# Edge-attribute loads of a graph layer: one group ahead in one burst, gated on the first scatter pair

## The reference, cut to what matters

```
row, col = edge_index                       # src, dst
tp  = fctp_messages(x[col], edge_attr, W1, W2, W3, W4)   # per edge: 160 features from x[col] and 32 attributes
messages = tp @ Wm + bm
agg = segment_sum(messages, row, num_segments=N_NODES)   # scatter-add over random src
upd = concatenate([x, agg], -1) @ Wu + bu
out = layernorm(x + x + upd)
```

## Time and profile before

| | |
|---|---|
| median of 3 runs | 1928.71 us (1927.19 to 1929.68) |
| the profiled execution | 1923.78 us, its span 1922.0 us |
| first scatter, last scatter, issued at | 139.77 us, 1679.95 us |
| DVE's first product (L493) of two groups 88 apart | 198.8 us, 1592.4 us |
| busy share of the span: PE, DVE, POOL, ACT | 86%, 81%, 56%, 47% |
| mean share of the DMA engines in use, loop | 0.76 to 0.79 |

### The profile page before, as it was taken

How to read it: one execution, slowest core, us unless ns; L and a number is a source line. 1 busy time by engine, 2 the same in 40 slices (tenths; PEclk the granted TensorE clock), 3 DMA queues, 4 the chain that set the end, 5 groups by cost and what they waited for, 6 DMA issues and landing times.

```text
span 1922.0 us, 35044 instructions
## 1 busy us (share of the span) xinstructions
PE 1660.2 (86%) x11964; PEld 894.9 (47%) x11964; DVE 1549.8 (81%) x1727; ACT 894.5 (47%) x1721; POOL 1079.2 (56%) x837
## 2 busy tenths in 40 slices
PE   5439999999999999999999999999999999378883
PEld 2214444444444444444444444444444444266662
DVE  6347888888888888888888888888888886089994
ACT  1204444444444444444444444444444444168885
POOL 3106666766666666666666666666666665301110
PEclk9779999999999999999999999999999999789997
DMA  9996777777777777777777777777777774799994
GB/s 378 405 377 181 232 232 226 231 230 230 230 228 231 231 230 231 229 230 231 235 234 236 235 237 234 237 225 239 239 234 235 231 230 99 237 361 420 418 412 178
DMA packets 174616, 490.06 MB, mean 255 GB/s; under 512 B 48664, under 2 KB 99096, under 8 KB 149484
## 3 DMA queue, kind: packets, MB, share of 16 engines
q1 hardware_dynamic: 91980, 379.42, 51.6%
q0 software_dynamic: 82304, 109.12, 27.3%
q10 hardware_dynamic: 288, 0.95, 0.2%
HBM read 393.10 MB, written 96.31 MB: 255 GB/s over the span
## 4 chain that ended last, share of the span: by engine, by line
DMA 39%; issue 20%; POOL 20%; PE 11%; DVE 5%; ACT 2%; SPq 1%; POOLq 1%; ACTq 0%; DVEq 0%
DMA agg<-summed,row_idx 25%; POOL agg L324 14%; POOL xg L307 6%; DMA prod<-agg 5%; DMA xg<-in_x_rows,dst_sb 4%; DMA agg<-start_rows 4%; PE ps L648 3%; PE ps L641 2%; DVE stats L585 2%; DVE prod L566 2%; DMA e_sb<-in_e_rep 1%; ACT spread L365 1%; PE ps L694 1%; PE ps L629 1%; PE ps L695 1%
## 5 line engine op out<-in xcount | busy, mean ns | idle before, releaser
L324 POOL DMA_INDIRECT agg<-summed,row_idx x392 | 642.2, 1638 | 448.9 <-DMA agg<-summed,row_idx 294.0
L505 DVE TENSOR_TENSOR prod<-ps,e_sb 128x2048 f32<-128x2048 f32 x294 | 663.7, 2285 | 136.8 <-PE ps L648 132.2
L648 PE MATMUL ps<-prod,packed_sb 128*32 128x512 f32 x3136 | 752.7, 603 | 0.8 <-ACT S_sb L377 0.8
L307 POOL DMA_INDIRECT xg<-in_x_rows,dst_sb x392 | 410.5, 1047 | 179.4 <-issue 117.8
L641 PE MATMUL ps<-prod,packed_sb 128*32 128x512 f32 x2352 | 394.3, 600 | 0.0
L365 ACT ACTIVATE spread<-xg 128x1536 f32<-128x1536 f32 x98 | 145.5, 1485 | 424.1 <-DMA xg<-in_x_rows,dst_sb 413.5
L513 DVE TENSOR_TENSOR prod<-ps,e_sb 128x3072 f32<-128x3072 f32 x98 | 328.1, 3348 | 0.0
L493 DVE TENSOR_TENSOR prod<-ps,e_sb 128x2048 f32<-128x2048 f32 x98 | 223.9, 2285 | 108.6 <-ACT A_sb L371 69.4
L648 PEld LDWEIGHTS ps<-prod,packed_sb 128*32 128x32 f32 x3136 | 148.6, 109 | 156.7 <-issue 156.7
L629 PEld LDWEIGHTS ps<-packed_sb,spread 128*128 128x128 f32 x1176 | 127.3, 143 | 172.2 <-issue 123.6
L377 ACT ACTIVATE S_sb<-ps 128x512 f32<-128x512 f32 x98 | 58.7, 599 | 277.8 <-PE ps L648 277.8
(11 more groups left out here) (62 smaller groups left out, 1748.6 us busy)
## 6 DMA issues: line engine op xcount, KB each, us to landing
e_sb<-in_e_rep SPq DMA_DIRECT2D x98, 1536.0 KB, 7.2
e_sb<-in_e_rep SPq DMA_DIRECT2D x98, 1024.0 KB, 5.6
agg<-start_rows SPq DMA_DIRECT2D x49, 640.0 KB, 17.1
prod<-agg SPq DMA_DIRECT2D x48, 640.0 KB, 10.7
out<-prod POOLq DMA_DIRECT2D x48, 640.0 KB, 7.7
row_sb<-in_src_row SPq DMA_DIRECT2D x98, 256.0 KB
prod<-in_x_t SPq DMA_DIRECT2D x25, 640.0 KB, 11.8
e_sb<-in_x_t SPq DMA_DIRECT2D x24, 640.0 KB, 12.9
```

The source lines that it names most:

```text
L307: nc.gpsimd.indirect_dma_start(xg[g[1] % 2][:, q, :], None, x_rows, bass.IndirectOffsetOnAxis(dst_sb[g[1]][:, q:q + 1].bitcast(U32), 0)).t ...
L324: nc.gpsimd.indirect_dma_start(agg, bass.IndirectOffsetOnAxis(row_idx[g[1]][:, q:q + 1].bitcast(U32), 0), summed[g[1]][:, q // 2, q % 2 * ...
L505: nc.vector.tensor_tensor(prod[g[1] % 2][:, 4 + 4 * i:8 + 4 * i, :].rearrange("p (a b) e -> p a b e", b=2), ps[:, t_bank(g, 1 + i), :].uns ...
L648: return nc.tensor.matmul(ps[32 * quarter:32 * quarter + 32, S_BANK, :], w[:, 32 * half:32 * half + 32], prod[g[1] % 2][:, tile, :], start ...
```

## The change

`load_e(g)` now is called for group s+1 in slot s, not for s+2, and only from slot 1 on (groups 0 and 1 are loaded ahead of the slots, as before). Its two transfers are issued one after the other with no wait between them. Ahead of the first stand a wait until DVE is through with group g-2, and from group 8 on a wait until the first pair of scatters of group g-4 has landed. For g = s+1 that is group s-3, the one whose scatters POOL issues in its slot s and whose `rows` DVE does in its slot s. Nothing else changes: the same transfers, the same sizes and buffers.

```
             def load_e(g):
                 if at_least(g, 2):
-                    sp.wait_ge(multiplied, number(g) * USES - 2 * USES + 4)
+                    sp.wait_ge(multiplied, (number(g) - 1) * USES)
+                    hold(sp, sp_passed)
+                if at_least(g, 8):
+                    sp.wait_ge(scattered, (number(g) - 4) * 64 + 32)
+                    hold(sp, sp_passed)
                 sp.dma_start(e_sb[g[1] % 2][:, 0:4, :], ...).then_inc(es_in[g[1]], 16)
-                if at_least(g, 2):
-                    sp.wait_ge(multiplied, number(g) * USES - 2 * USES + 6)
                 sp.dma_start(e_sb[g[1] % 2][:, 4:ET, :], ...).then_inc(ev_in[g[1]], 16)
...
-                if live(2):
-                    load_e(shift(s, 2))
+                if live(1) and at_least(s, 1):
+                    load_e(shift(s, 1))
```

## The result

| | before | after |
|---|---|---|
| median (lowest to highest), 4 runs each | 1927.95 us (1925.67 to 1929.68) | 2035.91 us (2032.3 to 2042.88) |
| ratio, 95% interval | | 1.0567 (1.0531 to 1.0604) |
| the profiled execution, its span | 1923.78, 1922.0 us | 2034.27, 2032.5 us |
| mean time of a group, from group 4 to group 94 | 15.79 us | 17.01 us |

What follows compares the result with a forecast made beforehand. POOL's scatter pairs, made long by attribute loads in flight, were taken to set the rate. The profiled execution summed to 1923.8 - 6 + 86 + 0 = 2004 us; the median, 4.9 us above, to 2010, range 1920 to 2055.

Steps and rivals of the forecast that it cites:

- steady term: Loop, 90 intervals of gated groups: a group takes 16.8 us instead of 15.84, +86 us (-31 to +140).
- the start: Before the loop: less load ahead of the last seven table pieces, so the first scatter goes earlier; -6 us (-12 to +10).
- The gate is what SP waits for last: SP's queue: the first pair of group s-3 always lands after `rows(s-3)`, for which `load_src` waits; the pair lands 5.3 us later.
- The loop through the gate costs nothing: Pair landed, load, `times_xs`, `rows`, POOL's restart, pair landed: 14.4 to 15.0 us, about the floor of 14.9.
- The burst is 0.8 us ahead of every second pair: SP issues both transfers 0.3 us after the first pair's landing, POOL the second pair at 1.1 us after it.
- Clear interval 6.42, hit interval 10.4: POOL's time from pair to pair: 6.42 us without a load, 10.4 (9.1 to 11.0) with both transfers on it.
- End, 0: Last scatter pairs: 16 `x_t` loads still fall on three of the last four pairs; 0 us (0 to +10).
- `times_xv` hides its load: DVE: the second transfer is through at 9.5 us after the landing, while PE holds DVE to 9 anyway; 1.9 us to spare.
- ACT's waits for gathers vanish: ACT: its waits for gathers go, since POOL must now be ahead; nobody gains, as PE then waits for DVE.
- No pair got in between the two transfers: Rival, second pair: scatters served between the burst's two transfers, interval 6.4 to 8, 1860 us; milder form 1885 to 1920; chance 0.18.
- The loop didn't bind: Rival: the gate's loop is longer than summed, PE's clock fall included; 17.5 us or more a group, 2070 and up; chance 0.07.
- The change moves nothing: Rival: gate long met when SP comes, or two pairs hit cost the same as one hit harder; 15.8 us, 1925; chance 0.05.

Runs made afterwards that it cites:

- e3: The changed kernel, but from group 8 on each transfer carries one attribute tile instead of four and six; 1832.87 us, ratio 0.9516.
- e10: The changed kernel with its gate on the landing of group g-4's second scatter pair instead of the first; 2518.56 us, one execution.
- e6: The changed kernel with DVE's `add_parts` cut to 8 of 512 columns, its sums left incomplete; 2039.67 us, ratio 1.0569 to the kernel before.
- e2: The changed kernel without the wait for the first scatter pair, `load_src` still ahead of the burst; 2073.36 us, ratio 1.0794.
- e5: The changed kernel without the wait for the first scatter pair, and with `load_src` called after `load_e`; 1972.59 us, ratio 1.0237.
- e1: The kernel before, two groups ahead and ungated, with both transfers waiting for the end of `times_y` and issued back to back; 1973.24 us, ratio 1.0246.
- e7: The kernel before, two groups ahead, with each transfer gated on a different scatter pair's landing and `load_src` between the two transfers; 1875.97 us, ratio 0.9733.
- e8: The changed kernel, its gate waiting for POOL's count placed behind a pair's second scatter instead of for a landing; 2131.14 us, ratio 1.1038.
- e11: The changed kernel, its gate waiting for POOL's count placed behind a pair of gathers instead of for a landing; 2193.22 us, ratio 1.1383.

## Why the prediction held, step by step

The sign and the place were right: 2036 us against 2010 in a range to 2055. Of the profiled execution it missed 30 us (2034.27 for 2004), 23 of them in the steady term and 6 at the start. The upper end of the range was drawn tighter than its own terms: with an interval of 10.9 us they give 90 x (17.3 - 15.84) = +131 on the median before, and with +10 at the start some 2070. The steps, in the order of the prediction:

- **The gate is what SP waits for last.** Right: in the waits of SP's queue from 200 to 1600 us the landing holds it 81 times, in each slot but one.
- **The loop through the gate costs nothing.** Right in its effect (e3, and e10 for what it looks like if it binds). From after's rows: landing 650.96, burst 651.18, and L497 starts at 656.81, 5.6 us later, at the upper end of my 5.1 to 5.7; the row numbers are done at 659.52, 3.0 us before the pair at 662.52 goes out. POOL's restart takes 0.8 of these, so 2.2 us of the 17.0 are slack, as the sum said.
- **The burst is 0.8 us ahead of every second pair.** Right in place, in size 1.3 us; e6 shows why, and that it hardly matters.
- **Clear interval 6.42, hit interval 10.4.** Measured 6.9 and 10.0. The stretched gather moves 0.5 us from one to the other and so cancels: what counts is the lag, 5.6 as forecast, and the block, 11.4 where I had 11.2. I had taken the near end for the pair's landing after the burst's issue, 10.4 us; it was 10.5 in the group shown.
- **Steady term, 90 x (16.8 - 15.84) = +86.** This is the mis-sized term. The rows give 1732.65 - 202.13 = 1530.5 us for the 90 groups from group 4 to group 94, and 1622.81 - 201.84 = 1421.0 before: +109.5. Of the 23.5 us missing, the block's 0.2 us a group is 18, and the period before, 15.79 instead of 15.84, is 4.5.
- **Start, -6.** The first half was right, the sum wrong. POOL's timeline of after:

```profile
133.66 1.62 POOL L328 DMA_INDIRECT agg<-summed,row_idx  x1 [38.42 <-issue]
...
147.78 1.61 POOL L328 DMA_INDIRECT agg<-summed,row_idx  x1 [0.30 <-issue]
...
162.24 1.61 POOL L328 DMA_INDIRECT agg<-summed,row_idx  x1 [8.35 <-DMA agg<-summed,row_idx]
...
168.65 1.61 POOL L328 DMA_INDIRECT agg<-summed,row_idx  x1 [0.30 <-issue]
...
182.79 1.61 POOL L328 DMA_INDIRECT agg<-summed,row_idx  x1 [8.03 <-DMA agg<-summed,row_idx]
...
202.13 1.61 POOL L328 DMA_INDIRECT agg<-summed,row_idx  x1 [0.30 <-issue]
```

The first scatter goes out 6.1 us earlier than before (139.77). But groups 2 to 7 have no gate, and the burst there follows the `src` row by half a microsecond (149.12 and 149.67 on SP's queue), as in e2: two intervals are 14.5 and 14.1 us long, and group 4 begins at 202.13, as late as before (201.84). In e5, with the row behind the burst, it begins at 195.33. The net is 0. I had priced the table's writes and not the first bursts.
- **End, 0.** Right: from 1732.65 us on after takes 60.7 us to its last landing, before took 60.6, from 1622.81 to 1683.4.
- **`times_xv` hides its load.** Wrong, without effect: DVE waited for it in 48 slots, 92.6 us in all, up to 3.1. DVE wasn't what set the rate.
- **ACT's waits for gathers vanish**, **one POOL wait a group**: right; POOL's waits were 4.0 us each and 327 in all, for 4.3 and 360.

Of the rivals, none happened. No pair got in between the two transfers: the shortest block of 70 groups was 11.0 us. The loop didn't bind, and the granted clock was 1.00 from 1200 to 1400 us. "The change moves nothing" fell with the steady term. What I had not seen is how the loss divides: the burst alone makes 46 of 108 us, and the gate most of the rest, since it holds the burst back until the clear pair has landed.

Open: why the block hardly depends on the lead, over 2.5 us, and in e2 over 4; whether a burst some 5 us ahead, with the `src` row elsewhere, would beat e1 and e5, since only e2 has such groups. e7's 15.3 us a group are near PE's floor of 14.8 (PE is busy 1169 of the 1200 us from 300 to 1500), and DVE still waits for attributes in it, 107 us at the product that uses the larger transfer first; what of the 0.5 us that is, no run tells. That taking turns with small packets is the whole reason for the block is a reading of the queues' rows. No run changed the packets' size.

## What to carry to other kernels

When small latency-bound DMAs (here scatter pairs that land 5.3 us after their issue) set the rate, don't count only how many of them meet a large transfer: price the time from the large transfer's issue to the landing of the one behind it, and add what comes before that issue. What did best here was to divide the large transfers, give each small one at most one of them, issued just ahead of it, and put middle-sized ones (the 256 KB row) beside the smaller half. A gate on a landing is an exact way to place a transfer but includes that landing's latency in every round.

## What the runs showed of the hardware that was not expected

- A semaphore that POOL counts up behind an indirect DMA in its program can rise before that DMA has begun: in e8 SP's issue at 692.00 us waited for a count that stands behind two scatters, the first of which began at 692.23; in e11 its issue at 690.62 waited for one that stands behind two gathers, the first of which began at 693.97. Such a count says how far POOL's program has come, not what has been issued.
- With a 256 KB transfer issued 0.7 us ahead of a 2.5 MB burst the block behind it was about 1 us longer (12.8 for 12.0), and the kernel 101 us slower than with the order reversed (e2 and e5; the wait that goes with the transfer moved too).
- DVE's 1.23 us add lengthened the POOL gather that ran into it from 1.0 to 1.4 us (up to 1.6), as e6 shows. In before a scatter took 2.29 us for 1.61 beside such an add (at 654.43 in the earlier trace rows; the add ran from 654.01 to 655.23), which no run tests.
